# Messages of a graph layer on one core: groups of 1024 edges, three bfloat16 parts, sums kept in PSUM

## The reference

```
ef  = relu(edge_attr @ We1 + be1) @ We2 + be2          # 64 -> 128 -> 128, per edge
ef  = ef * sigmoid(edge_weight * Wt + bt)
msg = relu(concat(x[src], ef) @ Wn1 + bn1) @ Wn2 + bn2
out = segment_sum(msg, dst)                            # per node
x   = layernorm(x + out + x)                           # as the reference nests it
```

## Time and profile before

| | |
|---|---|
| median of 3 runs | 9389.36 us (9377.11 to 9419.71) |
| span of the profiled execution | 9374.2 us |
| first and last gather of the message stage | 4711.2 and 9337.0 us |
| mean granted TensorE clock | 0.797 |

### The profile page before, as it was taken

How to read it: one execution, slowest core, us unless ns; L and a number is a source line. 1 busy time by engine, 2 the same in 40 slices (tenths; PEclk the granted TensorE clock), 3 DMA queues, 4 the chain that set the end, 5 groups by cost and what they waited for, 6 DMA issues and landing times.

```text
span 9374.2 us, 116910 instructions
## 1 busy us (share of the span) xinstructions
PE 6689.7 (71%) x36831; PEld 4954.1 (53%) x36831; DVE 4268.2 (46%) x9331; ACT 2188.8 (23%) x3195; POOL 5712.6 (61%) x5857
## 2 busy tenths in 40 slices
PE   4667777777656777767657777777777777777777
PEld 3455454444434555555545565565555555555555
DVE  6878777766634444444223233333333333333333
ACT  2111111111110000000023333333333333333333
POOL 6666555555546655655556666666666666666665
PEclk8788888888868888888767777777777777878777
DMA  3456666666647777777533333333333333333333
GB/s 101 128 174 204 200 225 227 221 223 217 223 136 254 243 252 250 257 245 252 192 121 118 109 112 117 109 117 113 110 118 114 110 112 123 112 114 121 113 118 93
DMA packets 585993, 1522.62 MB, mean 162 GB/s; under 512 B 148847, under 2 KB 362243, under 8 KB 558244
## 3 DMA queue, kind: packets, MB, share of 16 engines
q1 hardware_dynamic: 398177, 1131.24, 34.9%
q0 software_dynamic: 187200, 383.76, 14.7%
HBM read 1373.03 MB, written 141.47 MB: 162 GB/s over the span
## 4 chain that ended last, share of the span: by engine, by line
another core or an unknown queue 20%; PE 16%; issue 7%; DVE 4%; ACT 2%; DVEq 1%; DMA 0%; SPq 0%; ACTq 0%
PE messages_p_msg L1679 5%; PE messages_p_edge L1686 5%; PE messages_win L1696 4%; PE messages_p_hid L1673 3%; DVE messages_rows L1755 2%; ACT messages_hid L1711 1%; DVE messages_gated L1760 1%; ACT messages_gate L1715 1%; DVE messages_hot L970 1%; DVEq L62 0%; DVEq L1747 0%; DVE messages_sums L1750 0%; PE messages_win L1538 0%; ACT messages_rows L1719 0%
## 5 line engine op out<-in xcount | busy, mean ns | idle before, releaser
L1630 POOL DMA_INDIRECT messages_rows<-y_d,src_idx x3125 | 2992.2, 957 | 1694.2 <-issue 875.3
L1104 POOL DMA_INDIRECT sum_x_rows<-in_x,sum_x_edges x1525 | 1556.4, 1021 | 1084.4 <-PE sum_x_win L1194 514.6
L1104 POOL DMA_INDIRECT sum_z_rows<-z_d,sum_z_edges x1200 | 1162.6, 969 | 846.0 <-issue 322.4
L1679 PE MATMUL messages_p_msg<-Wm_e,messages_gated 128*128 128x128 f32 x6250 | 1127.9, 343 | 706.4 <-DVE messages_rows L1755 365.8
L1679 PEld LDWEIGHTS messages_p_msg<-Wm_e,messages_gated 128*128 128x128 f32 x6250 | 989.6, 244 | 1037.0 <-issue 996.4
L1755 DVE TENSOR_TENSOR messages_rows<-messages_p_msg,messages_rows 128x640 f32<-128x640 f32 x625 | 513.4, 821 | 1697.2 <-remote 1151.0
L1686 PE MATMUL messages_p_edge<-messages_hid,We 128*128 128x320 f32 x2500 | 1014.7, 539 | 254.7 <-DVE messages_gated L1760 128.3
L1206 PE MATMUL sum_x_build<-sum_x_key_hot,sum_x_low_hot 128*128 128x490 bf16 (+2 forms) x2900 | 869.6, 387 | 338.0 <-DVE sum_x_counts L1402 247.0
L1696 PEld LDWEIGHTS messages_win<-messages_hot,messages_rows 128*128 128x128 f32 x6250 | 947.0, 220 | 237.2 <-issue 164.9
L1696 PE MATMUL messages_win<-messages_hot,messages_rows 128*128 128x64 f32 x6250 | 909.1, 296 | 93.5 <-issue 67.5
L1711 ACT ACTIVATE messages_hid<-messages_p_hid,be 128x640 f32<-128x640 f32 x625 | 495.2, 792 | 1954.4 <-remote 1574.5
(11 more groups left out here) (250 smaller groups left out, 7916.5 us busy)
## 6 DMA issues: line engine op xcount, KB each, us to landing
sum_x_split<-x_parts_d SPq DMA_DIRECT2D x392, 675.5 KB
sum_z_split<-z_parts_d SPq DMA_DIRECT2D x392, 675.5 KB
messages_when<-in_edge_weight SPq DMA_DIRECT2D x125, 1600.0 KB
messages_attr<-in_edge_attr SPq DMA_DIRECT2D x125, 800.0 KB
counts_d<-sum_x_counts SPq DMA_DIRECT2D x28, 3136.0 KB
sum_z_counts<-counts_d SPq DMA_DIRECT2D x56, 1568.0 KB
messages_rows<-y_d,src_idx POOLq DMA_INDIRECT x3125
sum_x_rows<-in_x,sum_x_edges POOLq DMA_INDIRECT x1525
```

Source lines behind the costliest of these rows:

```text
L1104: nc.gpsimd.indirect_dma_start(out=rows[:, s % depth, j, :], out_offset=None, in_=table, in_offset=bass.IndirectOffsetOnAxis(ap=edges[:, b ...
L1630: nc.gpsimd.indirect_dma_start(out=rows[:, g % DEPTH, j, :], out_offset=None, in_=d["y"], in_offset=bass.IndirectOffsetOnAxis(ap=t.src_idx ...
L1679: last = nc.tensor.matmul(msg[:, j * P:(j + 1) * P], gated[:, g % GATEDS, j * P:(j + 1) * P], t.Wm_e[:], start=True, stop=True)
```

## The change

It rewrites the message stage:

- Groups have `SPAN` = 8 tiles, 1024 edges: 391 groups, the last one with 5 tiles. Attributes and weights are loaded per group (new arrays `span_attr`, padded `edge_weight`), four buffers, three groups ahead. PSUM tiles for hidden layer, second product and message are two full banks each.
- After the message addition, ScalarE writes the relu's high part as bfloat16 (`high_ready`); VectorE takes the rest, max(x, 0) minus high, in place in the room (`split_rest_ready`); ScalarE writes that as bfloat16 (`middle_ready`); VectorE writes rest minus middle as bfloat16 (`low_ready`). The three parts of a row stand side by side, 384 columns.
- GpSimd waits for `low_ready` (VectorE) instead of TensorE's window sums. There are 7 rooms of 8 tiles.
- The window sum is turned round: the one-hot of a tile (128 x 128, bfloat16) is the weights, the 384 columns of parts are the moving side; one matmul per tile.
- Its result stays in PSUM over a fixed run of tiles (a block, planned so that it covers about 113 nodes of the 128 in a window; 114 blocks, the first of 297 tiles, the last of some 14). At a block's end ScalarE copies 128 x 384 from PSUM, TensorE adds and turns the three parts by products with the identity (float32), and VectorE adds 128 x 128 to the node sums.
- The pieces' slots come from a new plan; two of their steps come a slot earlier.
- A check that all destinations lie in their block's window, and that no piece is taken before its blocks were added, sets the flag for the general version. It is made in slots 8 to 13.

Core of the diff (plan, loads, constants of the general version and the checks left out):

```diff
+SPAN, BLOCK_NODES = 8, 113
+SPAN_DEPTH, SPAN_PARTS, SPAN_HOTS = 7, 3, 3
+SPAN_LOADS, SPAN_AHEAD = 4, 3
+SPAN_HIDS, SPAN_GATES, SPAN_GATEDS = 2, 3, 2
+SPAN_MSG_LAG, SPAN_WIN_LAG = 2, 4
+SPAN_SPACING, SPAN_SOON, SPAN_CHECK = 3, 16, 12
...
-                wait_for(pool, sums_ready, g - DEPTH + 1)
+                wait_for(pool, low_ready, g - SPAN_DEPTH + 1)
                 pool.sem_inc(gathers_started, 1)
-                for j in range(TILES):
+                for j in range(tiles_of(g)):
...
+            def flip_block(b):
+                pe.wait_ge(block_copied, b + 1)
+                for i in range(SPLITS):
+                    last = nc.tensor.matmul(win[b % 2][:, 0:P], product[:, b % 2, i * P:(i + 1) * P], t.identity[:],
+                                            start=i == 0, stop=i == SPLITS - 1)
+                last.then_inc(block_flipped, 1)
...
+                    last = nc.tensor.matmul(win[b % 2][:, 0:SPLITS * P], hot[:, g % SPAN_HOTS, j, :], parts[:, g % SPAN_PARTS, j, :],
+                                            start=g * SPAN + j == begin, stop=g * SPAN + j == end - 1)
+                last.then_inc(win_summed, 1)
...
-                    for j in range(TILES):
-                        last = nc.tensor.matmul(win[g % 2][:, 0:WIN], rows[:, g % DEPTH, j, :], hot[:, g % WINDOW_HOTS, j, :],
-                                                start=j == 0, stop=j == TILES - 1)
-                    last.then_inc(sums_ready, 1)
...
+                for g in groups(s, SPAN_MSG_LAG + 1):
+                    act.wait_ge(rest_ready, g + 1)
+                    nc.scalar.copy(part(g, 1), room(g)).then_inc(middle_ready, 1)
...
-                    nc.scalar.activation(rows[:, g % DEPTH], rows[:, g % DEPTH], ACT.Relu).then_inc(msg_ready, 1)
+                    wait_for(act, win_summed, g - SPAN_PARTS + 1)
+                    nc.scalar.activation(part(g, 0), room(g), ACT.Relu).then_inc(high_ready, 1)
...
+                    nc.scalar.copy(product[:, b % 2], win[b % 2][:, 0:SPLITS * P]).then_inc(block_copied, 1)
...
+                for b in ended_at[s - 1] if s else []:
+                    add_block(b)
+                for g in groups(s, SPAN_MSG_LAG + 2):
+                    dve.wait_ge(middle_ready, g + 1)
+                    nc.vector.tensor_tensor(part(g, 2), room(g), part(g, 1), ALU.subtract).then_inc(low_ready, 1)
+                for g in groups(s, SPAN_MSG_LAG + 1):
+                    dve.wait_ge(high_ready, g + 1)
+                    nc.vector.scalar_tensor_tensor(room(g), room(g), 0.0, part(g, 0), ALU.max, ALU.subtract).then_inc(rest_ready, 1)
...
+                    nc.vector.tensor_tensor(at, p_msg[:, edges_of(g)], at, ALU.add).then_inc(msg_added, 1)
...
+                    nc.vector.scalar_tensor_tensor(gated[:, g % SPAN_GATEDS, :], p_edge[:], t.be2[:, 0:1],
+                                                   gate[:, g % SPAN_GATES], ALU.add, ALU.mult).then_inc(gated_ready, 1)
+                for g in groups(s, SPAN_WIN_LAG - 1):
+                    n = tiles_of(g)
+                    wait_for(dve, win_summed, g - SPAN_HOTS + 1)
+                    nc.vector.tensor_tensor(
+                        hot[:, g % SPAN_HOTS, 0:n], t.iota[:].unsqueeze(1).to_broadcast([P, n, P]),
+                        rel[:, g * SPAN:g * SPAN + n].unsqueeze(2).to_broadcast([P, n, P]), ALU.is_equal).then_inc(hot_ready, 1)
```

321 lines of the change are left out of this document (209 added, 112 removed).

## The result

The changed kernel takes 9527.51 us (median of 4 runs, 9491.42 to 9536.91) where the kernel before takes 9386.33 (9377.11 to 9419.71, the same three runs and one more): 1.0138 times as long, 95% interval 1.0118 to 1.0159. I had forecast 9140. The range (8760 to 9640) holds the time; the sign is wrong: some 250 us faster was forecast, 141 slower was measured. In the two profiled executions (9374.2 and 9489.7 us) the difference of 115.5 is -5 before the stage's first gather, 89 between its first and last gather, and 31 behind the last one. Of the 89, 73 fall in the last quarter of the tiles.

A forecast was written before the change was run, and what follows sets the result against it. Taken as bound: the chain TensorE, VectorE, ScalarE, with GpSimd only 15% from being the bound. Sum: 4711 + 390.6 groups x 11.2 (4375) + 37 = 9123, + 3 + 12 = 9138, say 9140 us; range 8760 to 9640.

The forecast's parts named there:

- GpSimd's floor and the held gathers: Message stage: gathers' floor 10.09 us per 1024 edges, plus 1.0 (0.5 to 1.5) held by VectorE's long two-SBUF-input instructions; 11.1 together.
- Stops: GpSimd's stops for a room in the message stage, 1.75 us per 1024 edges before, would have nearly gone.
- The end behind the last gather: Span after the message stage's last gather: 37 us as before the change, +-15.
- TensorE: Message stage, per 1024 edges: busy 8.75 us before, 8.7 after (7.6 at best); with idle time its path needs 10.6 to 11.8.
- The window: TensorE's window sum, eight bfloat16 matmuls of 384 columns per group: 2.4 us against 2.33 before, no gain; at best 1.1 saved.
- hand-offs: TensorE's idle time added to its path per group: 1.9 us if it belongs to the slot, 3.1 if to the edges.
- The fall of the clock: Warning for TensorE: were GpSimd the bound, its clock would fall to 0.50 more often; 12.0 us per group with every slot low.
- VectorE and ScalarE: Message stage, per 1024 edges: VectorE 6.7 us, ScalarE 5.3, both hidden behind GpSimd and TensorE.
- Loads, pieces, rooms: Edge and weight loads, pieces' steps and handing back of rooms: nothing; loads +-0.1 us per group, pieces 25 us if they showed.
- Rival C: Message stage: TensorE's path stays what it is per edge, 11.8 us per group, total 9372; chance 0.15.
- Rival D: Message stage: GpSimd's stops and held gathers add, 12.8 us per group, 9763; half the additions 12.3, 9568; chance 0.23.
- The late results: Message stage: while gathers run in a row at high clock, TensorE's results reach other engines late, bursting when GpSimd stops; unexplained.

The follow-up runs named there:

- e5: Changed kernel with nine phases of matmuls or round trips, alone and beside gathers, ahead of the message stage; beside gathers 0.16 us a pair, later 1.4 us an instruction.
- e9: Changed kernel with seven more phases beside 64 gathers, TensorE starting late or ScalarE alone; started 24.8 us after the gathers, TensorE got 45 pairs through before slowing.
- e14: Six phases beside 64 gathers, with real stops or held gathers; matmuls in second 15 us: plain 10, stop after 16 22, after 8 95, held 94.
- e10: The changed kernel run again unaltered, in rounds beside the kernel before the change; ratio 1.0193 to the kernel before.
- e7: Changed kernel with every second gather left out from the eighth group on; one run took 7686 us beside 9522.
- e16: Changed kernel with five rooms of 8 tiles instead of seven; ratio 1.0178 to the kernel before.
- e17: Changed kernel with GpSimd waiting after each group for its first seven tiles to arrive; pace 13.00 us per 1024 edges.
- e1: Changed kernel without VectorE's two row-splitting instructions (rest and low part), all waits kept; mean gather 0.989 us, total time not given in the text.
- e13: Changed kernel without ScalarE's copy and TensorE's six turning records at a block's end; ratio 1.0128 to the kernel before.
- e15: Changed kernel with the three bfloat16 parts undone (float32 window), plus 30 tiny ScalarE copies per group; pace 11.90 us per 1024 edges.
- e18: Changed kernel with the three bfloat16 parts undone (float32 window), GpSimd waiting after each group for its first seven tiles; ratio 0.9952 to the kernel before.

## Why the prediction was wrong

- **GpSimd's floor and the held gathers.** Right in mechanism, a little small: 1.0 forecast (0.5 to 1.5), 1.24 measured. GpSimd alone takes 11.26 for 11.1. The mean gather is 1.102 for "near 1.08".
- **Stops.** This is the step that failed. The prediction had the stops "nearly gone", because it took the larger of two resources, 11.1 and 10.6 to 11.8, as if each had its own time. They haven't: beside gathers in a row TensorE and ScalarE are cut off (e5, e9), and they get on when the gathers are stopped or held (e14). So 0.73 us of stops remain, 1.01 in e10. Over the 4715 us of the stage a group took 12.07, not 11.2: (12.07 - 11.2) x 390.6 = 340 us of the miss of 387. The end behind the last gather is 68 us for 37, another 31; the rest is the start (-5) and the distance from the span to the median (38 for 15).
- **TensorE.** The sum itself is off: 8.75 with 2.33 replaced by 2.4 and 0.35 added is 9.2, not 8.7. By the prediction's own rule the path was then 11.1 to 12.3 and not 10.6 to 11.8, which would have made TensorE the larger of the two; that would have come nearer, for a wrong reason. The window was mis-sized: 492.7 / 330 = 1.49 us per group for 2.4, near the other end of its bounds (1.3); the mean of the second stage's row was the wrong neighbour, half of it (1.2) the nearer one. Flips 112.6 / 330 = 0.34 for 0.35. Busy 7.35 for 8.7. With 1.4 us less work the pace rose, which speaks against TensorE's work as the bound. The idle time of 1.9 to 3.1 that I added as hand-offs is not that of hand-offs: in e7 a group takes 6.9 with 6.45 of them busy, 0.4 idle. The fall of the clock that the prediction warned of didn't come: 0.80 between 5000 and 9000 for 0.78 before.
- **VectorE and ScalarE.** 2016.8 x 8 / 2670 = 6.04 for 6.7, 4.67 for 5.3; hidden, as forecast.
- **Loads, pieces, rooms.** Costed at nothing; for the rooms e16 agrees. The others weren't tried. The end behind the last gather was put at 37 and took 68; nothing was run to take it apart.
- **Rival C** (11.8 per group, because the loss at the high clock stays) was the nearest: 11.8 to 11.9 in five of the eight stretches of 390 tiles of the changed kernel's stage (12.1 in the first, 12.6 and 12.7 in the last two, by the starts of the gathers). In e10 only one stretch is at 11.8. **Rival D** had the place right, interruptions that stay needed beside held gathers, and with half of its additions 9568 against 9527. That half of it fits is no test of its price: what speaks against it in the prediction, that "a held gather is itself a pause, in which results could come", is what e14 bears out. D added in full has about the pace of e17, 13.00 for 12.8, where the stops are planned ones.
- **The late results** I had before me in the earlier trace rows and called unexplained. I then let them fade into a chance of 0.23 instead of asking what the sum is if they persist: 10.02 + 1.8 = 11.8, that is no gain at all.

What stays open: why the kernels with the three parts have 2.0 to 2.6 us of interruptions, and those with the float32 window 1.8 to 1.9. It isn't VectorE's two instructions (e1) or the number of rooms (e16); the turning may be a part of it (e13). The window of 384 columns, ScalarE's second copy and the longer chain of hand-offs weren't taken apart. Nor is it known what fills and what empties: e15 speaks against a plain count of instructions, and the round trips of e5 say that VectorE's work hastens the cut-off. And one rival for the cut-off itself is untested: all executions here were recorded while they ran, so the recording of the instructions could be what slows them. That 30 more recorded instructions per group changed the pace by 0.05 (e15) speaks against its plainest form and doesn't settle it.

## What to carry to other kernels

When an engine is idle half of the time and yet everything waits for it, look for instructions with nothing to wait for that start microseconds apart; then suspect that two engines share something, and ask what the pace is as a sum and not as the larger of two busy times. Measure the chain once with the suspect thinned out (e7): it says in one run that 6.9 us were wanted where 12.0 to 12.3 were taken. Before taking work away from an engine beside long runs of gathers, ask what that work interrupts.

## What the hardware showed

- Beside gathers that follow one another every 1.25 us, TensorE and ScalarE work at full speed for 12 to 32 us and then perform one instruction per 1.4 us each until the gathers pause (e5, e9). VectorE's instructions of 1.22 us went on 1.26 apart. A pause of 1.5 us over the usual after 4 or 8 gathers, or 40 of 64 gathers held to 1.8 us, prevented it while TensorE had its 200 pairs to do, some 32 to 35 us; a pause after 16 didn't (e14), nor did one of 0.86 over the usual after 8 (e18). Whether an execution that isn't recorded does the same, these runs can't tell.
- A GpSimd that waits for the arrival of its own last gather loses 1.8 us, 1.5 more than its usual pause (e14); a hand-shake of 0.2 to 1.2 us with VectorE after 8 gathers is not seen in them at all (e9: all pauses stay at 0.305). A semaphore that GpSimd raises ahead of the 33rd gather came 24.8 us after the first one started, when only 20 had: its issue runs ahead of the gathers.
- VectorE instructions of 1.22 us with two inputs in SBUF, back to back, hold one gather (1.43) and none of the 63 behind it (e5). The Trainium skill (SBUF — State Buffer, "SBUF: two separate sides") has such an instruction and a GpSimd one that reads SBUF exclude each other for the whole instruction; the trace agrees where the two rhythms differ (e14: 40 of 64 gathers held to 1.8 us), and not where they are in step, with 63 gathers of at most 0.97 beside a VectorE that is hardly ever idle.
